# The order of the searches and weights in a decoder's second sublayer, and smaller blocks for the gated layer's scores

## The reference, cut to what matters

```python
# layer 2, per batch (512 text rows, 77 context rows, 4 heads of 32)
scores = einsum('bthd,bghd->bhtg', Q, K) / sqrt(32)
topv, topi = top_k(scores, 32)                  # 32 of 77, by row and head
attn_mean = scatter(softmax(topv)).mean(heads)  # [b, t, g]
c_t = attn_mean @ V
x = layernorm(x_text) * g_in + b_in
x = x * (1 + gate * scale_in(c_t)) + gate * shift_in(c_t)       # "film"
y = s4d(x)                                      # long convolution, by a DFT
y = y * (1 + gate * scale_out(c_t)) + gate * shift_out(c_t)
xt = x_text + y;  h = layernorm(xt);  xt = xt + gelu(h @ W1 + b1) @ W2 + b2

# gated layer, 8 heads, state S [64, 128]
S = a_t[..., None] * S + k_t[..., None] * v_t[..., None, :]     # per time step
o_t = einsum('bhcv,bhc->bhv', S, q_t)
out = o @ Wo.T + x
```

## Time and profile before

| | before |
|---|---|
| runs | 582.20, 580.77, 578.59 us |
| median | 580.77 us |
| profiled execution, its own time | 581.28 us |
| its span, first to last instruction | 579.5 us |
| PE busy | 479.7 us (83%), 4292 instructions |
| DVE busy | 420.3 us (73%), 1404 |
| ACT busy | 275.5 us (48%), 673 |
| POOL busy | 251.8 us (43%), 293 |
| mean granted clock of PE | 0.889 |

### The profile page before, as it was taken

How to read it: one execution, slowest core, us unless ns; L and a number is a source line. 1 busy time by engine, 2 the same in 40 slices (tenths; PEclk the granted TensorE clock), 3 DMA queues, 4 the chain that set the end, 5 groups by cost and what they waited for, 6 DMA issues and landing times. The chain is left out here.

```text
span 579.5 us, 12270 instructions
## 1 busy us (share of the span) xinstructions
PE 479.7 (83%) x4292; PEld 369.4 (64%) x4292; DVE 420.3 (73%) x1404; ACT 275.5 (48%) x673; POOL 251.8 (43%) x293
## 2 busy tenths in 40 slices
PE   3888792799599596799898999997999889689993
PEld 1565452486469564677593668775578645289983
DVE  4689949778997846865788999995697647237743
ACT  4599770430322245355412867562253413457741
POOL 3632499467902103355202443250577135516650
PEclk9978785589799885799999899979998979969998
DMA  8300004320000005706200000000472300251113
GB/s 250 121 2 1 1 2 148 89 94 2 2 0 1 2 26 135 130 1 111 40 1 0 1 2 2 1 2 2 183 314 67 88 0 34 60 144 48 47 48 103
DMA packets 27998, 33.39 MB, mean 58 GB/s; under 512 B 4961, under 2 KB 21073, under 8 KB 27426
## 3 DMA queue, kind: packets, MB, share of 16 engines
q1 hardware_dynamic: 26002, 29.13, 17.6%
q0 software_dynamic: 1504, 3.15, 1.6%
q10 hardware_dynamic: 432, 0.33, 0.2%
HBM read 26.44 MB, written 6.16 MB: 56 GB/s over the span
## 5 line engine op out<-in xcount | busy, mean ns | idle before, releaser
L2156 POOL TENSOR_TENSOR ea_scaled_rows<-ea_scaled_rows 128x768 f32<-128x768 f32 (+2 forms) x21 | 24.0, 1143 | 50.2 <-ACT ea_scaled_rows L2070 49.1
L3792 POOL DMA_INDIRECT em_results<-em_y_slot,slot_rows x31 | 29.7, 958 | 28.8 <-DVE em_y_slot L3919 28.2
L294 ACT ACTIVATE norm_log<-norm_var 128x4 f32<-128x4 f32 x20 | 4.1, 204 | 70.5 <-DVE norm_var L275 70.3
L3651 PE MATMUL banks<-em_slotT,em_weights 128*128 128x128 f32 x248 | 35.3, 288 | 2.6 <-ACT em_weights L3540 2.6
L3910 DVE SCALAR_TENSOR_TENSOR em_innerT<-banks,em_bias_of,em_soft 128x128 f32<-128x128 f32 x62 | 18.9, 346 | 22.7 <-ACT em_soft L3734 20.2
L38 PE MATMUL banks<-ea_w_high,ea_x_high 128*128 128x384 f32 x64 | 27.4, 428 | 8.6 <-DVE ea_acc L2247 8.5
L3651 PEld LDWEIGHTS banks<-em_slotT,em_weights 128*128 128x128 f32 x248 | 32.4, 204 | 3.3 <-issue 3.3
L2070 ACT ACTIVATE ea_scaled_rows<-banks,ea_gate 128x192 f32<-128x192 f32 x64 | 23.3, 418 | 18.7 <-PE banks L38 18.4
L2849 POOL TENSOR_TENSOR ga_sums<-ga_sums 128x512 f32<-128x512 f32 x8 | 9.1, 1136 | 42.8 <-DVE ga_sums L2910 42.8
L3734 ACT ACTIVATE em_soft<-banks,em_bias_of 128x128 f32<-128x128 f32 x62 | 19.4, 364 | 12.1 <-PE banks L3651 11.6
L38 PE MATMUL banks<-ea_w_low,ea_x_high 128*128 128x384 f32 x64 | 23.9, 373 | 0.0
(11 more groups left out here) (521 smaller groups left out, 1539.4 us busy)
## 6 DMA issues: line engine op xcount, KB each, us to landing
em_up<-in_em_up SPq DMA_DIRECT2D x3, 1536.0 KB, 12.1
ea_wide<-ea_gates SPq DMA_DIRECT2D x4, 1024.0 KB, 11.8
em_down<-in_em_down SPq DMA_DIRECT2D x3, 768.0 KB, 13.7
em_slots<-slot_rows SPq DMA_DIRECT2D x1, 2108.0 KB, 10.4
w_qkv<-in_w_qkv SPq DMA_DIRECT2D x1, 1536.0 KB, 7.3
slot_rows<-em_slots SPq DMA_DIRECT2D x1, 1360.0 KB, 8.5
cos_half<-in_cos_half SPq DMA_DIRECT2D x1, 1024.0 KB, 7.3
sin_half<-in_sin_half SPq DMA_DIRECT2D x1, 1024.0 KB, 9.5
```

Of the source, the lines that this page charges most:

```text
L2156: step(pool.tensor_tensor(scaled_rows[:, k, 0:n], scaled_rows[:, k, 0:n], scaled_rows[:, k, n:2 * n], ALU.add))
L3651: ins = pe.matmul(s.ps[:, k * P:(k + 1) * P], weights[:, n % NW, k // 2, k % 2 * P:(k % 2 + 1) * P], slotT[:, n], start=True, stop=True, s ...
L3792: pool.indirect_dma_start(core.results[:, :], bass.IndirectOffsetOnAxis(ap=slot_rows[:, s, P:P + 1].bitcast(U32), axis=0), y_slot[:, s % N ...
```

## The change

Three orders are changed, and no arithmetic.

On DVE, tile 5's search stands ahead of the film of half 0 and no longer behind it. On POOL, tile 3 is weighed before tile 2 is averaged; tile 5 is shifted and weighed before half 0's film is applied; tile 4 is weighed between the two bias additions; averages 4 and 5, the skip sum and half 1's affine follow later. DVE's average of tile 6 waits for POOL's average of tile 5, so that the count of finished means stays in order. In the gated layer each L2608 product of 128 keys by 128 queries becomes four products of 32 keys by 32 queries, the diagonal blocks alone.

```diff
@@ vector: average(g)
+            if g == LAST_AVERAGES:
+                dve.wait_ge(mean_ready, g)
             dve.wait_ge(total_ready, g + 1)
@@ gpsimd's order
-            for g in range(NT):
-                if g < NT - 1:
-                    two["weigh"](g)
-                if g == 3:
+            for g in range(HT):
+                two["weigh"](g)
+                if g == HT - 1:
+                    two["average"](HT - 2)
+                    two["average"](HT - 1)
                     two["affine"](0)
-                elif g == HT:
-                    for b in range(B):
-                        two["bias"](b)
-                    two["scale"](0)
-                elif g == HT + 1:
-                    two["affine"](1)
-                elif g == NT - 2:
-                    for n in range(2):
-                        two["split"](n)
-                if g + 1 < NT and g + 1 != HT:
-                    two["shift"](g + 1)
-                if g < LAST_AVERAGES:
+                two["shift"](g + 1)
+                if g < HT - 2:
                     two["average"](g)
-                if g + 1 == HT:
-                    two["shift"](HT)
-                elif g == HT:
-                    two["skip"](0)
+            two["bias"](0)
+            two["weigh"](HT)
+            two["bias"](1)
+            two["shift"](HT + 1)
+            two["weigh"](HT + 1)
+            two["scale"](0)
+            two["average"](HT)
+            two["skip"](0)
+            two["shift"](HT + 2)
+            two["weigh"](HT + 2)
+            two["average"](HT + 1)
+            two["affine"](1)
+            for n in range(2):
+                two["split"](n)
+            two["shift"](HT + 3)
@@ vector's order
             two["select"](4)
+            two["select"](5)
             two["film"](0)
-            two["select"](5)
             two["invert"](4)
@@ gated layer, PE mid
                     for p in range(NP):
-                        for n in range(2):
-                            pe.matmul(both[n].ps[:, p * P:(p + 1) * P], ks[own(n), K_MID, p], qs[own(n), Q_MID, p],
-                                      start=True, stop=True, skip_group_check=True)
+                        for e in range(NB):
+                            for n in range(2):
+                                some = slice(e * BLK, (e + 1) * BLK)
+                                at = both[n].ps[some, p * P + e * BLK:p * P + (e + 1) * BLK]
+                                pe.matmul(at, ks[own(n), K_MID, p, some], qs[own(n), Q_MID, p, some], start=True,
+                                          stop=True, skip_group_check=True)
```

## The result

The changed kernel is slower. Its first four executions took 588.07, 589.08, 586.90 and 587.89 us, median 587.98, against 580.67 of the kernel before beside them: ratio 1.0136, 95% interval 1.0095 to 1.0177. The prediction of 580.9 us (577.0 to 584.3) missed it. Twelve later executions gave 582.81 to 591.57 us, ratio 1.0060 [1.0029, 1.0091], which is 3.5 us. So a loss was measured both times, and the larger sample has the smaller one. The ratios compare executions within 1.5% of the fastest of their kernel; where the times of a kernel spread further, the plain medians of all its executions are given too.

A forecast was written before the change was run, and what follows sets the result against it. DVE's order was taken to bound layer 2, PE and POOL late by turns, and PE's score stage the gated layer's end. 581.28 + 2.0 (layer 2) - 1.9 (gated) = 581.4; median 0.51 lower: 580.9 us, range 577.0 to 584.3.

The forecast's parts named there:

- The chain of queues: Layer 2: half 0's transform waits for POOL's scale, behind tile 5's weighing, exponential 5 and ACT's scores copy; starts 142.8, not 137.97.
- 0.6 us at full clock: Layer 2's loss without any clock fall: search 7 starts at 153.0 instead of 152.41.
- Tile 3's early weighing: Layer 2, POOL: weighing tile 3 before averaging tile 2 removes DVE's wait before tile 3's sum, gaining all 1.09 us.
- the clock's term: Layer 2, PE: 4.2 us idle before the forward transform puts part of it at half clock, costing 1.7 us.
- The lengths of the half clock: Earlier trace, PE: between 3.0 and 4.5 us at half clock, costing 1.5 to 2.3 us.
- The sums beside POOL's work: Layer 2, DVE: four instructions behind the second wait, at 0.70 us each, take 2.8 us before search 7.
- DVE's added wait and the moved averages: Layer 2: later POOL averages are covered by tile 7's search, and DVE's wait for average 5 is met by some 153.
- The gated blocks: Gated layer: 64 small records take 0.54 us; tile 5 gains 0.85, tiles 6 and 7 0.55 each, together 1.9 us.
- The slower one, half clock twice: Rival, PE's two transforms: both at half clock, layer 2 + 3.7, gated - 0.2, 584.3 us; chance 0.17.
- The clock does not fall: Rival, layer 2: no half clock during or behind 4.2 us idle, + 0.6, gated - 1.9, 579.5 us; chance 0.18.
- Records as the pace of small products: Rival, gated layer: 15.2 ns per record whatever its columns, gated - 0.2 to - 0.3, 582.5 us; chance 0.08.
- the floor of about 25 ns: Gated layer, a page's estimate: products start at least 25 ns apart, 64 take 1.6 us, gated + 1.5, 584.3 us.

The follow-up runs named there:

- layer2_only: The changed kernel with the old 128x128 products back in the gated layer: ratio 1.0065 to the kernel before, +3.8 us.
- scale_first: The changed kernel with half 0's film applied on POOL ahead of tile 5's weighing: ratio 1.0012 to the kernel before, median 581.89 us.
- keep_warm: The changed kernel with unread products on PE in three idle times of layer 2, orders kept: ratio 1.0023 to the kernel before, +1.3 us.
- after: The changed kernel itself, nothing further altered, in its first profiled execution: 588.07 us.
- after_look_2: The changed kernel itself, nothing further altered, in the second of two later single profiles: 582.89 us.
- split_late: The changed kernel with POOL's two weight splits behind tile 7's shift: ratio 1.0195 to the kernel before, median 591.17 us.
- after_again: The changed kernel itself, nothing further altered, in the profile taken among its twelve later executions: 591.57 us.

## Why the prediction was wrong

- **The chain of queues was right, and its size at full clock too.** From search 4 I had 31.0 us to search 7 (122.0 to 153.0); with the clock held it was 30.87. The film's start 11.1 us after search 4, the copy of scores 6 4.11 us after that, 5.6 us to the transform (5.37) and 2.8 us behind the imaginary multiplication (2.83) all came so. The "0.6 us at full clock" was about 1.1, because of the next point.
- **Tile 3's early weighing was to gain all 1.09 us.** Its wait is gone, but from tile 1's sum to search 4 14.61 us passed against 15.05: 0.44 gained. In `layer2_only` and `scale_first` it is 1.08 and 1.16, but what they have more lies ahead of tile 2's sum; from there to search 4 every trace with the new order takes 4.93 to 4.96 us, with the old one 5.37 or 5.38. POOL's weighing now runs beside DVE's norm steps, and L281 takes 0.74 us where it took 0.26.
- **The step that failed is the clock's term**: it counted one gap of 4.2 us and one half clock, in part of the forward transform, at 1.7 us, and gave the film and the scores behind it no price at all. Measured against the held clock, A lost 2.2 to 5.2 us. In the first trace 1.6 of it lies in the film's last products and scores (5.75 us from the film's start to the copy, instead of 4.11), 1.9 in the transform (5.87 to the real half, with the clock held 3.98), 1.6 in DVE's two sums. The transform's price was right: 1.5 to 1.9 in the five traces of the changed layer 2. What was missing is the second gap. I had read the film's length from the earlier trace rows, where the third film product had not had to wait long; with the search ahead of the film PE idles some 3 us there, and what then runs slowly feeds exponential 5. In three of the five traces this cost 1.6 to 1.7 us, in the other two nothing.
- **The lengths of the half clock** in that term were misread, so that 1.7 came out right is in part luck: the 4.5 and 3.0 us of the earlier trace rows are the lengths of the windows that I had chosen. In the kernel before the granted clock was 0.50 from about 150.8 to 157.6 and from 198.6 to 208.8 us.
- **The sums beside POOL's work** were priced at the mean of 0.70 of before, although the second sum had taken 1.19 there. As the transform came late, they met half 1's affine and the splits: 4.43 us instead of 2.8 in the first trace, 3.42 to 3.53 in the other four.
- **DVE's added wait and the moved averages** cost nothing, as said: search 7 follows the second sum at once, and half 1's first multiplication comes 26.74 us after it (before 26.75 to 27.22).
- **The gated blocks** were to gain 1.9 us. Their stage is what I priced (0.56 us for 64, 8.75 ns each), and tile 7 gained its 0.55 (402.95 to the output product at 404.35 is 1.40 us, before 397.01 to 398.97, 1.96). Tile 5 gained 0.73 of its 0.85 (from DVE's copy of its scores to the value product 1.49 us, before 2.22). Tile 6's 0.55 was eaten by PE's stop behind it, which cost some 0.5 more. The layer was 0.8 us shorter, 1.3 with the blocks alone, and within 0.4 us of the old length in four traces where the half clock fell into its last 14 us. In the time nothing could be measured.
- **The rivals.** The slower one, half clock twice, had the right sign and the nearest time, 584.3 (the median of the twelve later executions is 584.84). That is luck, as its place was wrong. The backward transform did fall in the first trace (0.50 from 160.2 to 163.6), but from search 7 to half 1's first multiplication 26.74 us passed there and with the clock held alike; the fall that cost time stood in the film's products. "The clock does not fall" (579.5) is the case of keep_warm, 582.45. Records as the pace of small products are refuted by the 8.75 ns. With them falls the floor of about 25 ns from the Trainium skill's page "TensorE: Matmul & The Clock Gate", section "Wait — 56ns, not 53.3ns?", for this form of product.
- **The range.** The profiled execution was to take 581.4 us and took 588.07. Of the 6.7 us between, 3.8 lie in layer 2 (film 1.6, sums 1.6, tile 3 0.65), 1.1 in the gated layer, 1.0 ahead of tile 1's sum and 0.8 elsewhere; the range took the clock's fall as one event. That the first four executions lay at 587 to 589, and half of the next twelve near 583, is settled in part: between traces A differs by 3.0 us, what runs ahead of tile 1's sum by 4.0 and the gated layer by 4.4, and what set those times in the three executions without a profile is open.

## What to carry to other kernels

Before work is put ahead of a wait, follow the queue of every engine that the wait passes through: here four queues joined (DVE's film, PE's scores, ACT's exponential, POOL's scale), and one swap on one of them undid the loss as far as it can be measured. Then list every gap that the new order leaves on PE, not only the longest, and price each at the half clock together with what the delay slides it beside. A clock loss that differs from execution to execution is measured with the clock held, by the same kernel with unread products in the gaps.

## What the runs showed of the hardware

- DVE's sums with two operands in SBUF slow down while POOL's L1292 or L32 runs: 1.53 and 1.75 us beside them in `after`, 1.57 in `after_look_2`, 0.68 alone, and tile 6's average 1.26 and 1.18 instead of 0.32 and 0.24. POOL's instruction can grow as well (L1292 1.42 us in `after_look_2`, 1.09 in `split_late`). The multiplications, which read a PSUM bank, kept 0.69. The Trainium skill's page "SBUF — State Buffer", section "SBUF: two separate sides", has VectorE and GpSimd lock a pair of ports for a whole instruction, and names VectorE's operations with two SBUF inputs among those concerned; the trace agrees, with 1.57 us beside L1292 against 0.68 alone.
- PE's stops named "issue" keep their place among PE's instructions. They stand in front of the last 24 and 14 records of the farther-off blocks (L2628) in six of the eight traces with 4676 PE instructions, 0.26 to 0.94 us long; in the other two, `after_again` and `split_late`, whose gated layer is 3 to 4 us longer, there are none at these places. With 33 unread products ahead of them (keep_warm) they stand elsewhere, as here, in its lines L2629 and L2636:

```profile
354.64 0.23 PE L2629 MATMUL banks<-ga_faded 64*32 64x32 f32 x3 [0.79 <-issue]
372.37 0.21 PE L2636 MATMUL banks<-ga_faded 64*32 64x64 f32 x1 [1.31 <-issue]
```

  The page of the profile counts 38 packets on the queue of instructions, 35 before. That the place hangs on the number of PE instructions, and that a dense run of small products overtakes these transfers, is my reading; it was not tried by itself.
